# Int8 attention of a one-core network: order of ScalarE's roots, copies and pieces, and PSUM banks of the output projection

## The reference, cut to what matters

```python
x = x + xattn(layernorm(x), ctx, ...)      # 4: layernorm(z + summary) * gamma + beta
x = x + attn(layernorm(x), w_q, w_k, w_v, w_o, q_gain)   # 5
x = x + ffn(layernorm(x), ...)             # 6

def quant_matmul(x2, w):                   # both operands int8, scales by row
    w_scale = max(max|w| / 127, 1e-5);  wq = clip(round(w / w_scale), -127, 127)
    a_scale = max(max|x2| / 127, 1e-5); xq = clip(round(x2 / a_scale), -127, 127)
    return (xq @ wq.T) * (a_scale * w_scale)
def attn(x, ...):                          # 16 heads of 32, 4 key/value heads
    q, k, v = split(quant_matmul(x, concat(w_q, w_k, w_v)))
    q, k = rotary(rms_norm(q)) * q_gain, rotary(rms_norm(k))
    a = softmax(mask(q @ k.T / sqrt(32)))
    return quant_matmul(a @ v, w_o)
```

## Time and profile before

| | us |
|---|---|
| median of three runs | 898.15 |
| lowest and highest | 895.49, 899.02 |
| the profiled execution | 898.86 |
| its span in the trace | 897.0 |
| PE busy, share of the span | 816.8, 91% |
| DVE busy | 616.1, 69% |
| ACT busy | 490.1, 55% |

### The profile page before, as it was taken

One profiled execution on the slowest core, in us unless ns is written; L12 is line 12 of the kernel. 1 busy time (PEld: TensorE's weight loads), 2 busy tenths in 40 slices (PEclk: granted clock), 3 DMA queues, 4 the chain that ended last, 5 costly groups with the idle time before them and its releaser, 6 DMA issues.

```text
span 897.0 us, 13959 instructions
## 1 busy us (share of the span) xinstructions
PE 816.8 (91%) x5311; PEld 620.0 (69%) x5311; DVE 616.1 (69%) x1068; ACT 490.1 (55%) x817; POOL 169.8 (19%) x168
## 2 busy tenths in 40 slices
PE   3999999999799779999999998999977758999996
PEld 3897555778688568787887887445753537888885
DVE  6764885667764688999999986347787876333433
ACT  3565874333655587877787744445646535343331
POOL 2236540000254300000000000232131230212112
PEclk9999999999799799999999999999989758999999
DMA  8724566770133535434453005051034600212101
GB/s 309 251 107 161 177 204 251 262 246 30 34 105 104 172 117 165 140 98 127 131 165 106 12 25 192 0 196 39 1 98 175 253 1 24 69 50 71 48 1 47
DMA packets 49867, 106.80 MB, mean 119 GB/s; under 512 B 6714, under 2 KB 26098, under 8 KB 46220
## 3 DMA queue, kind: packets, MB, share of 16 engines
q1 hardware_dynamic: 48908, 95.33, 31.8%
q0 software_dynamic: 896, 10.62, 3.1%
HBM read 100.69 MB, written 5.25 MB: 118 GB/s over the span
## 4 chain that ended last, share of the span: by engine, by line
PE 82%; DVE 9%; ACT 5%; issue 2%; DMA 1%; SPq 0%; POOL 0%; ACTq 0%; DVEq 0%
PE banks L41 16%; PE banks L43 15%; PE banks L42 15%; PE banks L2161 6%; PE banks L364 2%; PE banks L2191 2%; PE banks L1728 2%; PE banks L1992 2%; PE banks L2192 2%; PE banks L1327 2%; PE banks L1357 1%; PE banks L1944 1%; PE banks L1188 1%; PE banks L1330 1%; ACT tw_wide L1908 1%
## 5 line engine op out<-in xcount | busy, mean ns | idle before, releaser
L157 POOL TENSOR_TENSOR w_low<-w_raw,w_high 128x256 fp32r<-128x256 f32 (+2 forms) x44 | 58.1, 1328 | 150.0 <-ACT w_high L153 149.9
L153 ACT CAST w_high<-w_raw 128x1024 fp32r<-128x1024 f32 (+2 forms) x74 | 56.8, 779 | 28.5 <-PE banks L43 22.7
L41 PE MATMUL banks<-da_xT_high,w_high 128*128 128x512 f32 x128 | 52.6, 411 | 1.4 <-DVE da_xT_low L210 1.4
L41 PE MATMUL banks<-hf_xhh,w_high 128*128 128x512 f32 (+1 forms) x136 | 51.8, 381 | 0.1
L43 PE MATMUL banks<-hf_xhh,w_low 128*128 128x512 f32 (+1 forms) x136 | 51.9, 382 | 0.0
L42 PE MATMUL banks<-hf_xhl,w_high 128*128 128x512 f32 (+1 forms) x136 | 51.9, 381 | 0.0
L43 PE MATMUL banks<-da_xT_high,w_low 128*128 128x512 f32 x128 | 50.9, 397 | 0.0
L42 PE MATMUL banks<-da_xT_low,w_high 128*128 128x512 f32 x128 | 50.7, 396 | 0.0
L2823 POOL TENSOR_TENSOR hf_hl<-hf_h,hf_hh 128x512 fp32r<-128x512 f32 x16 | 24.3, 1520 | 124.7 <-ACT hf_hh L2879 124.7
L2887 DVE TENSOR_TENSOR hf_downW_l<-dw_w,hf_downW_h 128x512 fp32r<-128x512 f32 x16 | 11.2, 697 | 50.7 <-ACT hf_downW_h L2839 50.7
L2041 POOL MEMSET ff_acc<- 128x512 f32 x1 | 0.5, 529 | 239.9 <-DVE x_res L1652 239.9
(11 more groups left out here) (439 smaller groups left out, 2495.4 us busy)
## 6 DMA issues: line engine op xcount, KB each, us to landing
cs_rows<-in_ctx SPq DMA_DIRECT2D x24, 1024.0 KB, 5.1
tw_raw<-in_L_ffn_w_gate_up SPq DMA_DIRECT2D x16, 512.0 KB, 4.4
hf_raw<-in_L_ffn_W_up SPq DMA_DIRECT2D x16, 512.0 KB, 3.5
w_raw<-in_L_xattn_W_o SPq DMA_DIRECT2D x8, 512.0 KB
w_raw<-in_L_attn_Wq SPq DMA_DIRECT2D x8, 512.0 KB
w_raw<-in_L_attn_Wk SPq DMA_DIRECT2D x8, 512.0 KB
w_raw<-in_L_attn_Wv SPq DMA_DIRECT2D x8, 512.0 KB
w_raw<-in_L_attn_Wo SPq DMA_DIRECT2D x8, 512.0 KB
```

Source lines behind the costliest of these rows:

```text
L41: nc.tensor.matmul(out, a[0], b[0], start=start, stop=False)
L153: self.nc.scalar.copy(self.wh[k][:, 0:cols], self.raw[k][:, 0:cols]).then_inc(self.split_hi[k], 1)
L157: self.nc.gpsimd.tensor_tensor(self.wl[k][:, 0:cols], self.raw[k][:, 0:cols], self.wh[k][:, 0:cols].bitcast(F32), ALU.subtract).then_inc(s ...
```

## The change

On ACT, first half: the two `quarter`s go ahead of the copies of scales; root 3 goes ahead of the copy of weight unit 0; root 5 and squares(0) ahead of units 3 and 4; three pieces instead of five stand ahead of quarter(2); `deviations(1)` stands behind piece 10 instead of behind piece 15. On ACT, second half: probabilities(0) go ahead of turned(3), the two `ffn.high` go behind them and to both sides of exponentials(1); probabilities(3) go ahead of the Sqrt table and of integers(2), root 6 behind outputs(2). On PE: probabilities(0) ahead of turned(3), probabilities(3) ahead of the matmuls of outputs(1), and the transposes of outputs are a step of their own. Outputs of quarters 1 and 2 use banks 0 to 3, free once DVE has subtracted the last maximum (`s_sub` 4); the waits on `y_read` are gone but for one. DVE's order is as before, and no operation is added or removed.

```diff
+    OUT_BANKS = ((4, 5), (0, 1), (2, 3), (4, 5))
...
-        self.weights.scalar_rows(act)
         act.wait_ge(self.set, 1)
         act.wait_ge(self.sa.rows_done, M)
         quarter(0)
         quarter(1)
-        self.weights.scalar(act, range(0, 1))
+        self.weights.scalar_rows(act)
         self.roots.scalar(act, 3, 2, 4)
-        self.weights.scalar(act, range(1, 3))
+        self.weights.scalar(act, range(0, 3))
         quarter_turned(0)
         quarter_turned(1)
         self.roots.scalar(act, 4, 2, 4)
+        self.roots.scalar(act, 5, 2, 4)
+        squares(0)
         self.weights.scalar(act, range(3, 5))
-        self.roots.scalar(act, 5, 2, 4)
-        pieces(0, 2)
-        squares(0)
-        pieces(2, self.turner.EARLY)
+        pieces(0, 3)
         quarter(2)
         quarter(3)
         squares(1)
         quarter_turned(2)
         quarter_turned(3)
         deviations(0)
-        pieces(self.turner.EARLY, self.turner.EARLY + 3)
+        pieces(3, 8)
         squares(2)
-        pieces(self.turner.EARLY + 3, self.turner.EARLY + 5)
+        pieces(8, 10)
         squares(3)
-        pieces(self.turner.EARLY + 5, FT)
+        pieces(10, 11)
         deviations(1)
+        pieces(11, FT)
...
         exponentials(0)
-        for t in range(2):
-            self.ffn.high(act, t)
+        probabilities(0)
         turned(3)
-        probabilities(0)
+        self.ffn.high(act, 0)
         exponentials(1)
+        self.ffn.high(act, 1)
         integers(0)
...
         exponentials(3)
+        outputs(1)
+        probabilities(3)
+        integers(2)
         self.roots.scalar_ready(act, ACT.Sqrt)
-        outputs(1)
-        integers(2)
-        probabilities(3)
+        outputs(2)
         self.roots.scalar(act, 6, 0, 2)
-        outputs(2)
         integers(3)
         outputs(3)
...
         def probabilities(m):
-            if m >= 2:
-                pe.wait_ge(self.y_read, m - 1)
+            if m == 2:
+                pe.wait_ge(self.y_read, 1)
...
+        def outputs_turned(m):
+            turn = self.OUT_BANKS[m][0]
+            pe.wait_ge(self.yq_ok, m + 1)
+            if m in (0, 3):
+                pe.wait_ge(self.at_out, 2 * min(m + 2, M))
+            else:
+                pe.wait_ge(self.s_sub, M)
+            for k in range(C): ...                       # four transposes to bank `turn`
+            ins.then_inc(self.yt_done, 1)
         def outputs(m):
-            pe.wait_ge(self.yq_ok, m + 1)
-            pe.wait_ge(self.at_out, 2 * min(m + 2, M))
-            if m:
-                pe.wait_ge(self.y_read, m)
-            for k in range(C): ...
-            ins.then_inc(self.yt_done, 1)
             pe.wait_ge(self.yt_out, m + 1)
             for k in range(C): ...                       # four matmuls to OUT_BANKS[m][1]
             ins.then_inc(self.y_done, 1)
...
         scores(1)
+        probabilities(0)
         turned(3)
-        probabilities(0)
         context(0)
         scores(2)
         probabilities(1)
         context(1)
+        outputs_turned(0)
         outputs(0)
         scores(3)
         probabilities(2)
         context(2)
+        outputs_turned(1)
+        probabilities(3)
         outputs(1)
-        probabilities(3)
         context(3)
+        outputs_turned(2)
         outputs(2)
+        outputs_turned(3)
         outputs(3)
```

More of the change, by code:

```diff
@@ L2375, in outputs @@
                 act.wait_ge(self.y_done, m)
-            nc.scalar.copy(self.yT[:, :, :], c.bank[:, 4, 0:256].bitcast(BF16).rearrange("p (c n) -> p c n", c=C)).then_inc(self.yt_out, 1)
+            nc.scalar.copy(self.yT[:, :, :], c.bank[:, self.OUT_BANKS[m][0], 0:256].bitcast(BF16).rearrange("p (c n) -> p c n", c=C)).then_inc(self.yt_out, 1)
         turned(0)
@@ L2486, in added @@
             dve.wait_ge(self.y_done, m + 1)
-            v.scalar_tensor_tensor(self.t[:, :], c.bank[:, 5, :], self.ysc[:, 1, m:m + 1], self.wsb[:, self.QKV:], ALU.mult, ALU.mult).then_inc(self.y_read, 1)
+            v.scalar_tensor_tensor(self.t[:, :], c.bank[:, self.OUT_BANKS[m][1], :], self.ysc[:, 1, m:m + 1], self.wsb[:, self.QKV:], ALU.mult, ALU.mult).then_inc(self.y_read, 1)
             dve.wait_ge(self.y_read, m + 1)
@@ L2652, in context @@
             ins.then_inc(self.o_done, 1)
-        def outputs(m):
-            pe.wait_ge(self.yq_ok, m + 1)
-            pe.wait_ge(self.at_out, 2 * min(m + 2, M))
-            if m:
-                pe.wait_ge(self.y_read, m)
-            for k in range(C):
-                ins = nc.tensor.transpose(c.bank[:, 4, 0:256].bitcast(BF16)[:, k * P:(k + 1) * P], self.yq[m % 2][:, k * P:(k + 1) * P], c.identb[:, :])
-            ins.then_inc(self.yt_done, 1)
+        def outputs_turned(m):
[5 more added lines that the diff above has]
+                pe.wait_ge(self.s_sub, M)
+            for k in range(C):
+                ins = nc.tensor.transpose(c.bank[:, turn, 0:256].bitcast(BF16)[:, k * P:(k + 1) * P], self.yq[m % 2][:, k * P:(k + 1) * P], c.identb[:, :])
+            ins.then_inc(self.yt_done, 1)
+        def outputs(m):
             pe.wait_ge(self.yt_out, m + 1)
             for k in range(C):
-                ins = nc.tensor.matmul(c.bank[:, 5, :], self.yT[:, k, :], self.wT[:, k, self.QKV:], start=(k == 0), stop=(k == C - 1))
+                ins = nc.tensor.matmul(c.bank[:, self.OUT_BANKS[m][1], :], self.yT[:, k, :], self.wT[:, k, self.QKV:], start=(k == 0), stop=(k == C - 1))
             ins.then_inc(self.y_done, 1)
```

## The result

The changed kernel takes 893.5 us in the median of 13 runs (892.36 to 895.57), the kernel before 898.15 (893.21 to 905.44). The ratio is 0.9956, with a 95% interval of 0.9939 to 0.9973. The time lies in the forecast range: 4.65 us faster by the medians, 4.0 by the ratio, where 5.9 were forecast, and on the line of 0.5%.

What follows compares the result with a forecast made beforehand. PE's chain of waits (82% of the span) was taken as the bound. Leads of 2.3 us up to context(2) grew to 5.89 at added(3), in sum 5.9 off the median 898.15: 892.2 us, range 889.0 to 895.8.

Steps and rivals of the forecast that it cites:

- The tail: From exponentials(3) to added(3): DVE is late next, and added(3) start at 731.05 us for 736.94, lead 5.89.
- At the slow clock throughout I get 5.9; I take that: PE over the whole changed stretch: slow clock assumed, eight transposes at 1.94 us rather than 1.09; total lead 5.9 us.
- The first rival: Middle and tail, 701 to 723 us: PE stays at full clock; lead 8.2 us, time 889.9 us; chance 29%.
- The rule that the prediction weighed against this rival: PE's dense stretch: transposes don't count as a busy PE for the clock, so it stays slow, time 892.2 us.
- The two `high` copies "stood in a gap and now stand in two others": ACT around exponentials(1): moving these copies (1.98 us) costs nothing; exponentials(1), behind the first, still lead by 1.6 us.
- The first half: Up to scores(0): root 3 leads by 2.1 us, pieces start 1.0 later, second projections lead 0.65, scores(0) lead 1.6.
- the second rival: First half: PE's clock falls in 3.7 us of idle time ahead of the pieces; lead 3.2, 894.9 us; chance 20%.
- Deviations(1): Ahead of scores(0): ACT's root comes out at 686.9 us, DVE's reciprocal starts at 688.9 without waiting for ACT, lead 1.9.
- The banks: Tail: separate banks are worth 1.35 us at outputs(3) and most of the 7.1 us by which probabilities(3) advance.
- the rival that they do little: Tail keeps its length, as DVE waits or POOL slows it; only 2.3 us from before it left, 895.8 us; chance 14%.
- POOL's mixing: Into the sixth block: it ends at 734.87 us for 739.32 and is covered by 0.2 us, so DVE decides.

Runs made afterwards that it cites:

- e5: Changed kernel with outputs of all quarters in banks 4 and 5 as before, with the waits this needs; ratio 0.9993 to the kernel before.
- e6: Kernel before with the four bank pairs and their waits alone, no order changed; ratio 0.9984 to the kernel before.
- e1: Changed kernel with both `ffn.high` copies moved on ACT from around exponentials(1) to behind integers(1); ratio 0.9938 to the kernel before.
- e2: Changed kernel with weight units 3 and 4 copied ahead of root 5 and squares(0) on ACT again; ratio 0.9941 to the kernel before.
- e9: Changed kernel with 22 unneeded matmuls on PE in the idle stretch ahead of the pieces; ratio 0.9943 to the kernel before.
- e11: Changed kernel with turned(3) ahead of probabilities(0) again on ACT and PE; ratio 0.9950 to the kernel before.
- e4: Changed kernel with the old ACT order of the first half, so the second half's changes alone; ratio 0.9969 to the kernel before.

## Why the prediction was right, and where it wasn't

The time was inside the range and the order of the tail was right, but the sum came out near by luck: against the forecast the lead lost 1.1 us up to scores(0), won 1.15 from there to context(0), lost 2.2 at POOL's subtraction and won 2.0 in the tail.

*The tail held, and was larger.* Forecast: probabilities(3) free of the read and of the Sqrt table, DVE late next, without a gap up to added(3). That is what the trace shows, from 720.64 us on. Probabilities(3) start 4.92 us earlier (+66.24 for +71.16), 7.1 less the 2.1 that had been lost ahead of them. It is the order that moves them, not the banks, to which the prediction gave most of it: in e5, with one pair, they start at +66.53, in e6, with the banks alone, at +70.53. But from context(2) to added(3) it took 12.69 us for 18.26, 5.57 less, where the steps gave 3.6. The step that was mis-sized is the clock: "At the slow clock throughout I get 5.9; I take that". TensorE ran at 1.00 from 716.5 to 726 us: probabilities(3) took 1.09 us for the forecast 1.94, and added(1) start 2.00 us behind the start of probabilities(3), not 3.85. The first rival's mechanism thus came in the tail, with 2.0 us for the 1.65 that it gave there, and ahead of context(0) too, where the transposes of probabilities(0) took 1.09 for 1.94; from scores(0) to context(0) it took 7.66 us, not 8.8. That context(0) led by 2.12, as forecast, is this gain against the first half's loss. The rule that the prediction weighed against this rival (the Trainium skill, TensorE: Matmul & The Clock Gate, Part 4: PE-mode transpose) isn't decided: in the tail eight transposes took 1.09 us, but among other matmuls at full clock.

*The two `high` copies "stood in a gap and now stand in two others"* is the step that failed. On ACT it is true. But every high copy releases a POOL subtraction of 2.4 us, and these moved from 699.95 to 701.71 us, while L2483 came from 706.73 to 704.03: they met. The lead of 2.12 at context(0) fell to -0.05 at scores(2). The step counted the moved instruction and not what it sets off on the engine behind it; e1 shows 2.2 us for it.

*The first half.* Root 3 and the quarters did as said. The idle time of PE was 5.55 us, not 3.7, since the earlier projections ran at full clock (2.54 us for 4.72) and PE was done sooner. The clock then fell, as the second rival said, the pieces cost 2.96 more, and the projections behind them, at full clock, gave 1.64 back: lead 0.47 at scores(0), not 1.6. That the wait is squares(0)'s and root 5's is shown by e2, that the slow pieces are the clock's by e9. Some of the missing lead is chance: e11, with the same first half, led by 1.5 at scores(0), its pieces being 1.35 faster.

*Deviations(1)* needed no wait for ACT, as said, and led by 0.46, not 1.9, for it inherits the late pieces.

*The banks* were worth 2.5 to 2.8 us, not 1.35, by e5 and e6; the rival that they do little is refuted. POOL's mixing came close but not last, as forecast: PE waited 1.46 and 2.19 us for it ahead of its transposes, and then 1.82 for DVE.

*What stays open:* the 0.77 us given back behind the stretch. From the first Hadamard matmul to the end the traces lie between 152.17 (e2) and 154.20 (e4), with no order by version, so I put it to the runs' spread. And the granted clock of a trace is read, not forecast: nothing here says why the same idle stretch cost 1.4 us more in one version than in another. The forecast's chances leaned to more than 0.5%, and the result is at that line.

## What to carry to other kernels

Count of a moved instruction also what it releases: here two copies moved by 2 us put GpSimd's subtraction on a VectorE operation and cost 2.2 us, what the middle had won. An instruction that waits should not be put ahead of one that is ready and that TensorE needs, even if its own chain gains; the idle time costs twice when the clock falls behind it. Where an engine stops in the middle of equal work, look at the transfers beside it, and at the packets of the instruction queue.

## What the runs showed of the hardware that was not expected

- A VectorE fp32 tensor_scalar from SBUF to SBUF (128x512, 0.49 us) beside a GpSimd subtraction of 128x1024 fp32 took up to 2.70 us, and ended 0.28 to 0.29 us behind it in the five traces in which it met the second one.
- Twenty-two unneeded matmuls in an idle stretch brought the next five needed ones from 7.5 to 4.56 us.
- TensorE stopped for 3.56 us between equal transposes at 403 GB/s of transfers, and for 0.94 us at the same place without any; both times it went on 1.3 to 1.4 us behind the end of a 16 KB packet of the instruction queue.
